# An adaLN and expert layer on one core: VectorE's order of adding tanh, computing slots and normalising in the front rounds

## The reference, cut to what matters

```python
x = x + tanh(rotate(x, delta_t, amplitudes, frequencies) @ W @ W1 @ W2 + bias)
z = relu(hidden @ Wd[profile] + bd)
y = hidden + z @ Wu[profile] + bu
y = (y - mu) * rsqrt(var + eps) * g + b
expert_idx = argmax(y @ Wr.T + br)
out = x + (relu(y @ W1[e].T + b1[e]) @ W2[e].T + b2[e])   # e = expert_idx of the token
```

## Time and profile before

| what | value |
|---|---|
| median of 3 runs | 160.32 us (160.28 to 160.7) |
| the profiled execution's own time | 160.17 us |
| its span | 158.3 us |
| TensorE busy | 139.8 us (88%) |
| VectorE busy | 117.4 us (74%) |
| GpSimd busy | 104.2 us (66%) |
| ScalarE busy | 75.3 us (48%) |

### The profile page before, as it was taken

The page is one execution under the profiler, slowest core; times in us unless marked ns, Lnnn a source line. Parts: engine busy times, 40 slices in busy tenths (PEclk is TensorE's granted clock), DMA queues, the critical chain, the costliest instruction groups (busy, mean ns, idle before and its releaser), DMA issues.

```text
span 158.3 us, 4649 instructions
## 1 busy us (share of the span) xinstructions
PE 139.8 (88%) x1183; PEld 133.0 (84%) x1183; DVE 117.4 (74%) x494; ACT 75.3 (48%) x230; POOL 104.2 (66%) x150
## 2 busy tenths in 40 slices
PE   5959898899999975599799299999999999999991
PEld 5849798898898965598697199999999999999891
DVE  1589636879999799778974357778878877877750
ACT  3488685675765507233454123444444444444330
POOL 6967432326787777887787885566556557557554
PEclk9999999999999999659999969999999999999998
DMA  4868687759999522625378443343343334234200
GB/s 113 185 189 208 205 214 215 203 124 268 376 407 395 187 101 71 198 81 161 107 227 253 134 117 97 88 115 102 91 107 105 89 95 112 84 102 125 69 26 0
DMA packets 19365, 24.32 MB, mean 154 GB/s; under 512 B 4321, under 2 KB 15587, under 8 KB 19218
## 3 DMA queue, kind: packets, MB, share of 16 engines
q1 hardware_dynamic: 14898, 17.37, 38.1%
q0 software_dynamic: 2832, 6.50, 12.0%
q10 hardware_dynamic: 1616, 0.21, 0.9%
HBM read 16.51 MB, written 8.01 MB: 155 GB/s over the span
## 4 chain that ended last, share of the span: by engine, by line
PE 56%; POOL 14%; issue 12%; DVE 6%; ACT 4%; DMA 4%; SPq 1%; DVEq 1%; POOLq 0%; ACTq 0%
PE bank L763 14%; PE bank L752 14%; POOL expert_rows L418 7%; PE bank L644 5%; POOL out L433 4%; PE bank L672 4%; PE bank L663 4%; PE bank L633 4%; DMA rows<-expert_rows 4%; PE bank L709 3%; ACT zT L543 3%; PE bank L694 2%; PE bank L611 2%; PE bank L741 2%; POOL ids L429 1%
## 5 line engine op out<-in xcount | busy, mean ns | idle before, releaser
L433 POOL DMA_INDIRECT out<-res,ids x39 | 38.8, 995 | 15.9 <-issue 13.6
L752 PE MATMUL bank<-tileT,stage 128*128 128x128 f32 x312 | 43.8, 285 | 3.0 <-DVE hT L1128 3.0
L560 ACT ACTIVATE hT<-bank,stage 128x128 f32<-128x128 f32 x78 | 24.4, 364 | 45.7 <-PE bank L752 45.7
L752 PEld LDWEIGHTS bank<-tileT,stage 128*128 128x128 f32 x312 | 39.9, 200 | 4.2 <-DVE hT L1128 3.2
L763 PE MATMUL bank<-w_s,hT 128*128 x312 | 42.4, 280 | 0.0
L418 POOL DMA_INDIRECT expert_rows<-payload,slot x32 | 32.3, 1010 | 12.8 <-issue 7.4
L763 PEld LDWEIGHTS bank<-w_s,hT 128*128 128x128 f32 x312 | 38.7, 195 | 0.3
L1113 DVE TENSOR_SCALAR stage<-w_s 128x644 f32 x36 | 19.9, 553 | 9.4 <-issue 4.5
L1128 DVE TENSOR_SCALAR hT<-bank,stage 128x128 f32<-128x128 f32 x66 | 20.0, 344 | 5.1 <-PE bank L752 4.5
L1183 DVE TENSOR_TENSOR res<-bank,resid 128x128 f32<-128x128 f32 x39 | 10.9, 280 | 6.5 <-DMA out<-res,ids 4.5
L555 ACT ACTIVATE tileT<-bank 128x128 f32<-128x128 f32 x39 | 10.9, 279 | 7.3 <-PE bank L741 7.3
(11 more groups left out here) (129 smaller groups left out, 210.3 us busy)
## 6 DMA issues: line engine op xcount, KB each, us to landing
rows<-expert_rows SPq DMA_DIRECT2D x39, 130.0 KB, 2.1
cond_s<-in_cond SPq DMA_DIRECT2D x32, 130.0 KB, 2.3
w_s<-in_w SPq DMA_DIRECT2D x1, 2064.0 KB, 9.9
x1T<-in_xT SPq DMA_DIRECT2D x8, 256.0 KB, 3.4
w_s<-in_w SPq DMA_DIRECT2D x1, 2048.0 KB, 16.8
expert_rows<-pad SPq DMA_DIRECT2D x8, 130.0 KB, 2.9
out<-res,ids POOLq DMA_INDIRECT x39
w_s<-in_b SPq DMA_DIRECT2D x1, 512.0 KB, 11.3
```

The lines of the kernel that those rows point to most:

```text
L433: pool.indirect_dma_start(out=out_rows, out_offset=bass.IndirectOffsetOnAxis(ap=ids[:, i:i + 1], axis=0), in_=res[:, k, :], in_offset=None ...
L560: op = nc.scalar.activation(hT[:, k, c * P:(c + 1) * P], ps_lo[:, c * P:(c + 1) * P], ACT.Relu, bias=stage[:, k, FF + c:FF + c + 1])
L752: op = nc.tensor.matmul(half[:, c * P:(c + 1) * P], stage[:, k, c * P:(c + 1) * P], tileT[:, k, :], start=True, stop=True)
```

## The change

The three instructions of `find_slot`, the one of `add_x` and the four of `normalise` change places at the end of VectorE's round. In rounds 4 to 7 `add_x` comes ahead of `find_slot`, and `normalise` stays last. In rounds 8 and 9 (where there is no `add_x`) `normalise` comes ahead of `find_slot`. No instruction is added or removed, and the other engines' queues keep their order.

```diff
                 if building:
                     build_rot(built, 2)
                     build_rot(built, 3)
-                if routing and routed < GROUPS - 2:
-                    for part in range(3):
-                        find_slot(routed, part)
                 if ADDED_EARLY <= t < GROUPS:
                     if t == ADDED_EARLY:
                         dve.wait_ge(s_x1T, ADDED_EARLY)
                     add_x(t)
-                if norming:
+                if norming and t >= GROUPS:
+                    normalise(normed)
+                if routing and routed < GROUPS - 2:
+                    for part in range(3):
+                        find_slot(routed, part)
+                if norming and t < GROUPS:
                     normalise(normed)
```

## The result

| kernel | runs | median, us (lowest to highest) | ratio to before, 95% interval |
|---|---|---|---|
| before | 12 | 160.3 (158.31 to 161.91) | |
| changed | 12 | 160.7 (159.46 to 161.82) | 1.006 (1.0032 to 1.0088) |
| changed, timed again | 12 | 161.37 (159.48 to 163.75) | 1.004 (0.9992 to 1.0087) |
| before, timed as if it were a change | 12 | 160.03 (158.76 to 163.41) | 0.9973 (0.9931 to 1.0015) |

The profiled execution took 160.22 us (span 158.3), against 160.17 (158.3) before. Medians in the tables are over all runs, while ratios, their intervals and the comparisons of times in the text leave out the runs in the chip's slower state. The runs of one kernel differ by 2 to 5 us, more than the change is worth, so the total alone says only that it is the same or a little slower: +0.4 us by the medians, 1.0 us by the ratio.

A forecast was written before the change was run, and what follows sets the result against it. GpSimd's queue up to the first scatter of group 6 was taken as the bound: round 8 +1.2, slack -0.9, rounds 4 to 7 +0.05, rounded to +0.3 us on 160.32, giving 160.6 us; range 159.7 to 161.4.

The forecast's parts named there:

- Round 8, slots of group 4 1.2 us later: VectorE's round 8: payloads ahead of the slots make GpSimd, already waiting for these slots, get them 1.2 us later.
- the 0.20 us before the first payload: Round 8 on VectorE: the first payload was to start 0.20 us behind the start of tile_r, at 61.11.
- GpSimd's slack of 0.90 us: GpSimd ahead of the first scatter of group 6: it could have started at 74.67 instead of 75.57, 0.90 us.
- the queue behind the late scatter: GpSimd's later instructions, from group 4's other scatters to the row ids at 74.32, all move by 1.2 us.
- Round 9, half of VectorE's wait used because rstd is late: Round 9: payloads fill VectorE's 0.95 us wait but need the delayed rstd; VectorE wins 0.5 us, the end nothing.
- Rounds 4 to 6, +0.10 each: VectorE's rounds 4 to 6: add_x ahead of find_slot costs +0.10 us a round, 0.3 us in all.
- round 7 gives them back: Round 7: add_x in VectorE's 0.76 us prefix wait wins 0.25 us, so VectorE enters round 8 at +0.05.
- The collisions are moved and not removed: GpSimd's long instructions beside VectorE's work: taken as 0, with bounds of +0.47 and -0.74 us.
- A: Rival: VectorE's hidden waits in rounds 7 and 9 are worth more than the late slots; 159.6 us, chance 0.15.
- B: Rival, scatters of groups 4 to 6: GpSimd pays the whole delay and one collision more (+0.47); 161.4 us, chance 0.32.

The follow-up runs named there:

- 8 and 9: Kernel before with normalise ahead of the slots in rounds 8 and 9 alone, rounds 4 to 7 as before: 160.55 us, ratio 1.0046.
- the first set: Four kernels, each the one before with tanh ahead in rounds 4 to 7, or normalise ahead in 8 and 9, 8, or 9: 160.53, 160.55, 160.6, 159.41 us.
- the best one: Kernel before with tanh added ahead of the slots in round 7 and normalise ahead in round 9 only: 159.3 us, ratio 0.9937.
- 8 alone: Kernel before with normalise ahead of the slots in round 8 only: 160.6 us, ratio 1.0028.

## Why the prediction was right, and where not

The forecast was "the same, on its slower side", +0.3 us by one path through GpSimd. The medians gave +0.4 (160.3 to 160.7), the marks +0.43 at the scatter of group 6 and +0.24 at the last row ids. The path is the one that the traces show. That the size came out as near is partly luck: a delay sized 0.2 us too large, longer row ids that were put at nothing, and a shorter scatter behind them offset one another. Point by point:

- **Round 8, slots of group 4 1.2 us later: right in kind, 0.2 us too large.** It was 1.00 us in both traces (1.07 with normalise alone). The term that was mis-sized is the 0.20 us before the first payload: behind tile_r it took 60.37 - 60.29 = 0.08, which makes 1.07. The other 0.07 is that the slots come 0.07 earlier with tanh ahead, as in the kernel with that half alone (31.05). The 0.20 are seen behind slot, which waits for its predecessor, in both kernels; that this wait makes the difference isn't tested.
- **GpSimd's slack of 0.90 us, and the queue behind the late scatter: right.** From the first scatter of group 4 to that of group 6 it took 12.79, 12.81 and 12.90 us in three traces without a wait between, against 12.79 worked out, and 13.08 with normalise in round 8 alone, where the row ids took 0.52. In the profiled changed kernel it was 13.22, with row ids of 0.53 where the sum had 0.20. So the queue took 0.11 and 0.43 us more than worked out in the two traces of the changed kernel, against a forecast of nothing, and with 1.00 - 0.90 that makes +0.20 and +0.53 against the first trace of before, or +0.43 between the means.
- **Round 9, half of VectorE's wait used because rstd is late: right.** Payload waited 0.68 us for rstd and began 36.08 us from the mark (36.2 forecast). The 0.5 us at the end of the round came in one trace (37.76 instead of 38.32) and only 0.1 in the other (38.21), where VectorE waited 0.31 us for TensorE's transposes (L683). What the prediction passed over is why TensorE is late in round 9: its queue stands at the first row load, and neither the prefix nor the transposes behind it can start. That wait was 1.55 us before and 3.06 in the first trace of the changed kernel (2.28 in the second, where the load came 0.80 us earlier from the mark).

```profile
66.40 0.30 PE L741 MATMUL bank<-route_ident,rows 128*128 128x128 f32 x1 [3.06 <-DMA rows<-expert_rows]
```

- **Rounds 4 to 6, +0.10 each, and round 7 gives them back: right to 0.03 us.** 0.09, 0.20, 0.30, and then +0.02 at round 8 (0.05 forecast). What I passed over is the other side: the scatters that come 0.4 us later there were costed at nothing. In the kernel with rounds 4 to 7 alone GpSimd entered group 4 0.39 us late, which its slack behind it still covered. In the whole change this is hidden, as GpSimd waits for the slots of group 4 anyway.
- **"The collisions are moved and not removed": wrong by place and by trace.** The long row ids above were new. Behind the scatter of group 6 the first trace of the changed kernel needed 12.85 us to the last row ids instead of 13.19 and 13.17, as a long scatter fell away (see below); the second needed 13.13, with long instructions at other places. In the mean that took the +0.43 down to +0.24. So the end doesn't simply move by what the start of that scatter moves by.

Of the rivals, A (hidden waits outweigh) fell for this change. The price is round 8's: with the move in round 9 alone the scatter of group 6 is at 44.69, with 8 and 9 at 45.44. With round 9 and round 7 moved, and rounds 4 to 6 and 8 as before, A holds (44.36, and a total 0.6% lower). B (a whole collision more, +0.47) didn't come, though a part of it did in the row ids. The last 70 us show no plain order. From the last row ids to the start of the last store it took 66.95, 67.35, 65.90, 66.62, 68.24, 66.37 and 66.36 us in the first traces of before, changed, and the kernels of the first set and the best one, and 66.91 and 67.22 in the second traces of before and changed. So between the two main kernels 0.3 to 0.4 us are added here, which the prediction ruled out: the last store starts 125.41 and 125.23 us from the mark before, and 126.00 and 125.82 in the changed kernel, +0.59 in the mean. The places where they part are TensorE's wait near 88 us (2.84 to 3.00 before, 3.91 and 3.58 changed) and, ahead of it, VectorE's wait for a store to land (3.94 and 3.80 before, 5.31 and 4.49 changed):

```profile
89.53 0.29 DVE L1185 TENSOR_TENSOR res<-bank,resid 128x128 f32<-128x128 f32 x1 [5.31 <-DMA out<-res,ids]
```

Why it is longer stays open; in the traces of the other six kernels from sessions with 160 us it is 3.45 to 4.30 us. Part of the spread in the seven numbers above is TensorE's clock: behind the last row ids it was at 0.50 for 6.8 us in the trace with 68.24, and in the last one not at all before 155.8 us of the trace.

## What to carry to other kernels

Before moving a step that another engine waits for, work out that engine's slack behind it and what else stands in its queue: here 1.0 us of delay against 0.9 of slack turned two filled waits into nothing. Put a step ahead of another only in the rounds where the other really waits (7 and 9 here), not in all rounds of a kind. Where runs of one kernel differ by more than the change is worth, compare traces from a mark ahead of the change, and time the old kernel against itself.

## What the runs showed of the hardware

**The start decides 2.4 us.** In three of the ten traces from sessions with 160 us, round 4 began at 32.25 to 32.44 us, in the other seven at 29.73 to 30.30. Those three executions took 160.96, 162.2 and 162.55 us, the other seven 158.29 to 161.22, so part of the spread between runs comes from here. Timeline of TensorE, first the second trace of before, then that of the changed kernel:

```profile
6.93 1.13 PE L633 MATMUL bank<-wp,x1T 128*128 128x128 f32 x8 [0.70 <-DMA br_s<-in_br]
```

```profile
7.11 2.05 PE L633 MATMUL bank<-wp,x1T 128*128 128x128 f32 x8 [0.28 <-DMA br_s<-in_br]
9.91 2.08 PE L644 MATMUL bank<-rot,u 128*128 128x128 f32 x8 [0.75 <-ACT u L523]
```

And the busy time of that second trace of the changed kernel in this stretch (columns as in the earlier trace rows):

```profile
4.00:10.00 6.00, 4.97 (x28) 4.11 (x26) 3.50 (x19) 3.01 (x8) 5.58 (x4) 1.00 0.77 190
```

The same eight multiplications took 1.13 us in one and 2.05 in the other, while the granted clock reads 1.00, full speed. Half the pace until about 14 us is what the later start of round 4 is made of: behind it the same step (L694) starts at 16.70 us instead of 14.04, and the 2.7 us are still there at round 4. Why one execution has it and another doesn't stays open.

**Where GpSimd's long instructions come from.** Wherever GpSimd had waited for the slots of group 6, its fourth scatter behind them took 1.43 to 1.46 us, in all five such traces, and it needed 13.17 to 13.21 us to the last row ids; where it hadn't, that scatter took 1.15 or 1.16 us in four traces of five, and 12.85 or 12.86 us. The changed kernel:

```profile
80.59 0.48 DVE L1113 TENSOR_SCALAR stage<-w_s 128x644 f32 x1
80.76 1.16 POOL L418 DMA_INDIRECT expert_rows<-payload,slot  x1 [0.30 <-issue]
```

VectorE's copy begins 0.17 us before the scatter here and 0.13 us behind its start before. The scatter ends 0.85 us behind the end of the copy in both: 81.92 against 81.07 here, 82.28 against 81.43 before. It is 0.83 to 0.85 in nine of the ten traces. In the tenth, the second of the changed kernel, the copy came and went ahead of that scatter, which took 0.96 us. The row ids fit a wait for the copy too. At 74.87 they took 0.53 instead of 0.20 and ended 0.04 us behind a copy that ran from 74.86 to 75.36, and in the three other kernels with a copy beside these row ids (8 and 9, 8 alone, 7 and 9) they ended 0.03 or 0.04 us behind it. The Trainium skill ("SBUF — State Buffer", "SBUF: two separate sides") has a VectorE copy in its two-port mode and GpSimd lock each other out of a shared port pair for the whole instruction. That these copies run in that mode no view shows. The row ids and the fourth scatter agree with it, while the scatter of 0.98 us at 82.67 with a copy from 82.71 still doesn't. No run here took the copy away, so the cause is argued and not shown.

**TensorE's clock falls in round 9.** In all ten traces the granted clock falls from 1.00 to 0.50 (2.4 to 1.2 GHz) 34.6 to 37.7 us behind the start of round 4. TensorE waits 1.20 to 3.06 us for the first row load there; in the first trace of before the clock falls within that wait, in the other nine behind it. The changed kernel on both sides of the fall, columns as in the earlier trace rows:

```profile
62.70:66.70 4.00, 0.94 (x11) 0.69 (x10) 3.29 (x21) 0.98 (x2) 3.47 (x4) 1.00 0.59 164
66.70:70.10 3.40, 3.30 (x23) 2.92 (x22) 2.27 (x15) 0.90 (x3) 2.62 (x7) 0.50 0.24 84
```

The prediction has no term for it. The runs suggest that it costs the changed kernel something: of 75 runs of the kernel before in the sessions with 160 us that have their clock on record, 17 have a mean granted clock of 0.984 or more (median 159.04 us), of the 19 of the changed kernel none. At a mean clock of 0.97 to 0.979 the medians are 159.73 us (31 runs) and 160.28 (12), so about 0.5 us of the loss is there at an equal clock. That the longer wait of TensorE for the row load is what keeps the clock from staying up is argued from these rows; no run moved the load alone.
